# A loop over routed attention tiles: 33 tiles always and then pairs up to 39, in place of 32 always and then pairs up to 40

## The chip, the cores and the metric

The kernel runs on one core of a Trainium2 chip. The metric is the device time of one execution in microseconds. Three runs of the kernel before the change took 3995.53, 3995.71 and 4000.58 us; their median is 3995.71 us.

## What is computed

The reference is a sequence of eight sublayers over 2048 tokens of 128 channels, each added to its own input. The change lies in the sixth, a mixture of attention experts. For every token a small router picks two of eight experts. Each expert is a full attention over all 2048 tokens with 16 heads of 8 channels and its own weights; what it gives for a token is weighted by the router's gate. Cut to what matters:

```
probs = softmax(relu(layernorm(x @ rW1.T + rb1)) @ rW2.T + rb2)
tp, ti = top_k(probs, 2); tp = tp / tp.sum(-1)
for each expert e:                       # eight of them
    q, k, v = x @ W{q,k,v}[e].T + b      # 2048 tokens, 16 heads of 8
    o = softmax(q k^T * 8**-0.5) v
    out += (o @ Wo[e].T + bo[e]) * gate[token, e]   # gate 0 where e wasn't picked
```

An expert's output matters only for the tokens that picked it, so the kernel computes attention only for these (token, expert) pairs: 2 x 2048 = 4096 query rows in all.

## The kernel before, in words

**Lists and tiles.** `l2_router` counts how many tokens each expert got, and gives every expert as many tiles of 128 query rows as it needs, the last one of each filled up with blanks. The tiles of all experts stand one behind the other. `end[:, E - 1]` (lines 2173 to 2181) is the number of tiles needed. It lies between 32 (4096 / 128, nothing wasted) and 39. The list of query rows by tile is written to HBM by `l2_prepare`: first every entry is blanked with 0 (line 2289), then each pair's row is scattered to its slot (L2293). A blank entry thus means row 0. `l2_prepare` also computes queries, keys and values of all eight experts and stores them in HBM.

**The loop.** `attention_loop` (called by `l2_ffn` with `routed`) then works through the tiles. The instructions are written out for each tile and each engine; `each_tile` (lines 427 to 443) decides how many run. The first 32 bodies always run. Then every engine loads the number of rounds, which the router has computed, and two bodies at a time stand behind a comparison of it (L440): 16 rounds are the 32 tiles, and each round more is a pair of tiles, up to 40. So an even number of tiles runs, the smallest that holds those needed; a tile too many is computed from blanks and its result isn't used. The router's side is a chain on VectorE (lines 2179 to 2183): for each possible round n, is `end` greater than 2n, added up.

**One tile.** For 16 heads and all 2048 keys: a first pass of matmuls for the scores (TensorE, L666) whose maxima VectorE takes from PSUM (L908, 32 a tile), a second pass that gives the scores less their maximum (L691, 256 a tile), exponentials on ScalarE (L846, 64 a tile), and the weighted sum of the values (L712, 512 a tile). The first pass runs three of four groups of heads ahead of the second. Then a division on VectorE, two transpositions and the projection with the expert's output weights (L736), copied to `y` (L864) and stored by SyncE (L540). GpSimd splits the maxima and queries into bfloat16 parts (L598 to L605), loads the list of tile i + 2 (L1966) and gathers its queries with an indirect DMA (L1970); the gathered rows are transposed by TensorE (L749). SyncE loads keys (L288), values (L509), query parts (L480) and the maximum's rows (L489) for the tiles i + 1 and i + 2, whichever experts they belong to. Buffers alternate with the parity of the tile.

**The end.** The last step's values (L712), the division, transpositions and projection of the last tile stand behind the loop and go by the loaded number of tiles. SyncE waits there for every load it has issued, GpSimd for its gathers. `l2_collect` gathers each token's two results (L2407) from `expert_y_dram`, whose rows for tiles that might not run were blanked before (L2286).

Of the kernel before, what the change touches and what calls it, by code (L numbers as in the profile page):

```python
# [24 lines left out]
ALU = mybir.AluOpType  # L25
# [3 lines left out]
P = 128  # L29
T = 2048  # L30
# [367 lines left out]
def attention_loop(c, at, lead, tri=None, routed=None, keys_placed=None):  # L398
# [13 lines left out]
    tiles = routed.tiles if routed else NT  # L412
# [14 lines left out]
    def each_tile(eng, body):  # L427

        if not routed:
            for i in range(tiles):
                body(i)
            return tiles
        for i in range(2 * routed.least_rounds):
            body(i)
        rounds = eng.value_load(routed.rounds[0:1, 0:1], min_val=routed.least_rounds, max_val=tiles // 2)
        for r in range(routed.least_rounds, tiles // 2):
            with eng.If(rounds > r):  # L440
                body(2 * r)
                body(2 * r + 1)
        return rounds * 2

    def kx(tile):
        return at.kx[:, tile % 2 if routed else 0]
# [4 lines left out]
    q_loaded = [c.sem(f"attn_q_loaded{k}") for k in range(2)]  # L451
# [7 lines left out]
    if routed:  # L459
        k_loaded = [[c.sem(f"attn_k_loaded{k}{g}") for g in range(G)] for k in range(2)]  # L460
        v_loaded = [c.sem(f"attn_v_loaded{k}") for k in range(2)]
# [3 lines left out]
    QL = 16 * (2 * NR if routed else 2)  # L465
    KL = 16 * 2 * 2
# [3 lines left out]
    with nc.Block() as block:  # L470
        @block.sync
        def _(sp):
# [85 lines left out]
                load_max(g, 0)  # L558
            done = each_tile(sp, routed_loads if routed else tile_loads)
            if routed:  # L560
                pieces_ahead, pieces_placed = (done + 2) * (KL // 2), done * (KL // 2)
                sp.wait_ge(y_stored, done * 16)
                for g in range(G):
                    sp.wait_ge(max_loaded[g], done * ML + (ML if g < 2 else 0))
                for k in range(2):
                    sp.wait_ge(v_loaded[k], pieces_placed if k else pieces_ahead)
                    for g in range(G):
                        sp.wait_ge(k_loaded[k][g], pieces_placed if k and g == 3 else pieces_ahead)
                for k in range(2):
                    sp.wait_ge(q_loaded[k], done * (QL // 2) + QL)  # L570
                sp.wait_ge(s2_read, ring.read_when(done, 4))
                sp.dma_start(routed.y_dram[bass.ds(done, 1)].rearrange("a p d -> (a p) d"), routed.y[:, :]).then_inc(last_y_stored, 16)
                sp.wait_ge(last_y_stored, 16)
            else:
                for k in range(2):
                    sp.wait_ge(q_loaded[k], tiles // 2 * QL)
                for g in range(G):
                    sp.wait_ge(max_loaded[g], tiles * ML)

        @block.gpsimd  # L580
        def _(pool):
            g_ = nc.gpsimd

            class Link:


                def __init__(self):
                    self.k = 0

                def __call__(self, ins):  # L590
                    self.k += 1
                    ins.then_inc(pool_chain, 1)
                    pool.wait_ge(pool_chain, self.k)

            def same(dst, src):

                ones = at.one[:, :] if len(src.shape) == 2 else at.one[:, :].unsqueeze(2)
                return g_.tensor_tensor(dst, src, ones.to_broadcast(list(src.shape)), ALU.mult)  # L598

            def split(src, parts, rest, link, ready):  # L600

                link(same(parts[0], src))
                link(g_.tensor_tensor(rest, src, parts[0], ALU.subtract))
                link(same(parts[1], rest))
                g_.tensor_tensor(parts[2], rest, parts[1], ALU.subtract).then_inc(ready, 1)  # L605

            link = Link()

            def split_max(g, tile):
                pool.wait_ge(negm_ready, tile * G + (g + 1))  # L610
                split(at.negm[:, 4 * g:4 * g + 4].rearrange("p (a j) -> p j a", j=2), [at.mparts[:, g, :, n, :] for n in range(3)],
                      at.rest[:, g, :].rearrange("p (j a) -> p j a", j=2), link, mparts_ready)

            def split_q():
                split(routed.qT[:, :], [routed.qparts[:, n, :] for n in range(3)], routed.qrest[:, :], link, qparts_ready)

            if routed:
                for k in range(2):
                    if k:
                        pool.wait_ge(q_loaded[0], QL)  # L620
                    pool.wait_ge(first_q_copied, k + 1)
                    split_q()
            for g in range(lead):
                split_max(g, 0)

            def whole_tile(i):
                if routed:
                    routed.load_index(pool, i + 2, i % 2)
                for g in range(G):
                    group, tile = first_pass_of(i, g)  # L630
                    if routed and g == 0:
                        pool.wait_ge(routed.list_loaded, i * 16 + 48)
                        routed.gather(pool, i % 2)
                    if routed and g == 2:
                        pool.wait_ge(q_loaded[(i + 1) % 2], ((i + 1) // 2 + 1) * QL)
                        pool.wait_ge(s2_read, ring.read_when(i, ring.place(i, "q")))
                        split_q()
                    if exists(tile):
                        split_max(group, tile)

            done = each_tile(pool, whole_tile)
            if routed:
                for k in range(2):
                    pool.wait_ge(routed.gathered[k], done * 8 + 16)

        @block.tensor
        def _(pe):
# [1285 lines left out]
class Routed:  # L1933
# [7 lines left out]
    def __init__(self, c, ctx, E, K):  # L1941
        nc, sb = c.nc, c.sb
        self.E = E
        self.tiles = (K * T + E * (P - 1)) // P + 1
        self.listed = self.tiles + 2
        self.least_rounds = K * T // P // 2
        self.rounds = sb(ctx, "rounds", [1, 1], mybir.dt.int32)
        self.expert_of = sb(ctx, "expert_of_tile", [1, self.listed], mybir.dt.int32)
        self.q = sb(ctx, "gathered_q", [P, 2, P], F32)
# [43 lines left out]
def l2_router(c, ins, rt, E, K, gate, slot, row, y_row, fixed):  # L1993
# [3 lines left out]
    with ExitStack() as ctx:  # L1997
# [14 lines left out]
        first, end, index = c.sb(ctx, "first_tile", [P, E], F32), c.sb(ctx, "end_tile", [P, E], F32), c.sb(ctx, "partition", [P, 1], F32)  # L2012
        many = c.sb(ctx, "many", [P, 2], F32)
# [20 lines left out]
        with nc.Block() as block:  # L2034
# [83 lines left out]
            def _(dve):  # L2118
                v = nc.vector
# [56 lines left out]
                link(v.tensor_reduce(of_tile[:, :], passed[:, :], X, ALU.add))  # L2176
                v.tensor_scalar(of_tile[:, :], of_tile[:, :], float(E - 1), None, ALU.min).then_inc(of_tile_ready, 1)

                link(v.memset(many[:, 0:1], float(rt.least_rounds)))
                for n in range(rt.least_rounds, rt.tiles // 2):  # L2180
                    link(v.tensor_scalar(many[:, 1:2], end[:, E - 1:E], 2.0 * n, None, ALU.is_gt))
                    link(v.tensor_tensor(many[:, 0:1], many[:, 0:1], many[:, 1:2], ALU.add))
                link(v.tensor_copy(rt.rounds[:, :], many[0:1, 0:1]))

# [18 lines left out]
def l2_prepare(c, at, ins, rt, slot, row):  # L2203
# [6 lines left out]
    E, K = rt.E, 2  # L2210
    with ExitStack() as ctx:
# [1 line left out]
        bq, bv, bk = c.sb(ctx, "b_q", [P, 2, P], F32), c.sb(ctx, "b_v", [P, 2, P], F32), c.sb(ctx, "b_k", [P, 2], F32)  # L2213
        bq_ordered = c.sb(ctx, "b_q_head_order", [P, P], F32)
        wT = c.sb(ctx, "wT_qkvo", [P, 2, 4, P], F32)
        used = 2 * rt.least_rounds + 1
        blank_y, y_blanked = c.sb(ctx, "blank_y", [P, P], F32), c.sem("p_y_blanked")
        blank = c.sb(ctx, "blank_list", [rt.listed, P], mybir.dt.uint32)
        start = c.sb(ctx, "p_start_credit", [P, 10], F32)
# [559 lines left out]
```

## Time and profile before

| | us |
|---|---|
| median of three runs | 3995.71 |
| the profiled execution | 3996.37 |
| its span, first to last instruction | 3994.6 |
| TensorE busy in the span | 3278.7 (82%) |
| VectorE busy | 3026.2 (76%) |
| ScalarE busy | 2560.2 (64%) |
| GpSimd busy | 579.2 (14%) |
| mean granted clock of TensorE | 0.912 |

The profile is that of one execution; its times are us from the first instruction. PE is TensorE's matmuls and PEld its weight loads, DVE VectorE, ACT ScalarE, POOL GpSimd, SP SyncE; a "q" behind an engine's name means its sequencer, which branches, waits and issues DMAs while the engine itself stands idle. "L712" is a line of the kernel. An arrow `a<-b` reads "a written from b". "issue" as a releaser means that the engine waited for nothing that the profile shows. Names with `l2f_` belong to the sublayer of this change; the first sublayers use the same lines without it.

### The profile page before, as it was taken

What the parts mean: (1) busy time and instruction counts of PE and PEld (TensorE: products, weight loads), DVE (VectorE), ACT (ScalarE), POOL (GpSimd) and SP (SyncE); (2) the same over time, 40 slices, a digit from 0 to 9 for tenths busy, and PEclk for the clock granted to TensorE, in tenths of its full rate; (3) what the DMA queues carried; (4) which work ended last, traced back from release to release, by engine and by line L of the source; (5) the groups of instructions that cost most, each with busy time, mean ns of one, the idle gap of its engine ahead of it and who ended that gap; (6) DMA issues with size and microseconds to landing.
All of it is one profiled execution on the core that took longest, in us unless ns stands there. A gap on an engine that the chain in (4) does not pass through costs nothing. (4 is left out here: it accounts for less than half of the span.)

```text
span 3994.6 us, 130089 instructions
## 1 busy us (share of the span) xinstructions
PE 3278.7 (82%) x55226; PEld 2129.2 (53%) x55226; DVE 3026.2 (76%) x3768; ACT 2560.2 (64%) x4943; POOL 579.2 (14%) x1529
## 2 busy tenths in 40 slices
PE   2999999489997996464945559999999999999728
PEld 1666666235555674122434426666666666666414
DVE  5999999358893114997353459999999999999753
ACT  1899999347776343332211139999999999999622
POOL 0000000011000000563012011111111111111120
PEclk7999999779998998898957769999999999999858
DMA  4000000300000000530009864555545455455410
GB/s 115 9 7 9 9 7 5 98 17 11 9 7 2 22 21 27 179 137 6 1 22 172 243 157 118 127 125 123 128 122 130 120 128 127 120 126 120 107 34 11
DMA packets 209577, 305.80 MB, mean 77 GB/s; under 512 B 93116, under 2 KB 137602, under 8 KB 207950
## 3 DMA queue, kind: packets, MB, share of 16 engines
q1 hardware_dynamic: 202270, 286.06, 28.4%
q10 hardware_dynamic: 2048, 6.29, 0.8%
q8 instruction: 430, 7.05, 0.8%
q0 software_dynamic: 4688, 5.24, 0.6%
q14 instruction: 141, 1.16, 0.1%
HBM read 228.17 MB, written 60.40 MB: 72 GB/s over the span
## 5 line engine op out<-in xcount | busy, mean ns | idle before, releaser
L846 ACT ACTIVATE channels_qk<-psum 128x512 f32<-128x512 f32 (+1 forms) x3906 | 2101.0, 593 | 287.6 <-PE psum L691 201.8
L908 DVE TENSOR_REDUCE l2f_chunk_max<-psum 128x2 f32<-128x1024 f32 x1176 | 1359.7, 1218 | 53.2 <-PE psum L666 49.4
L908 DVE TENSOR_REDUCE chunk_max<-psum 128x2 f32<-128x1024 f32 (+2 forms) x832 | 918.6, 1158 | 105.5 <-PE psum L666 57.6
L666 PE MATMUL psum<-l2f_k_parts,l2f_q_parts 48*128 48x512 bf16 x2352 | 715.9, 388 | 37.7 <-DVE l2f_chunk_max L908 26.3
L691 PE MATMUL psum<-l2f_q_parts,l2f_k_parts 51*128 51x128 bf16 x9224 | 728.1, 218 | 3.7 <-issue 2.7
L712 PE MATMUL psum<-channels_qk,l2f_v_and_ones 128*9 128x128 f32 x18432 | 718.5, 274 | 13.3 <-issue 13.0
L691 PEld LDWEIGHTS psum<-l2f_q_parts,l2f_k_parts 51*128 51x128 bf16 x9224 | 496.9, 94 | 43.2 <-ACT channels_qk L846 38.9
L666 PE MATMUL psum<-k_parts,q_parts 48*128 48x512 bf16 (+3 forms) x1664 | 425.8, 382 | 109.6 <-DMA q_parts<-q_rows_dram 72.2
L712 PE MATMUL psum<-channels_qk,v_and_ones 128*9 128x128 f32 x12544 | 493.8, 276 | 1.7 <-ACT channels_qk L846 0.5
L712 PEld LDWEIGHTS psum<-channels_qk,l2f_v_and_ones 128*9 128x9 f32 x18432 | 396.8, 90 | 122.0 <-issue 15.7
L691 PE MATMUL psum<-q_parts,k_parts 51*128 51x128 bf16 x6272 | 431.4, 219 | 29.3 <-DMA q_parts<-minus_max_rows 10.4
L666 PEld LDWEIGHTS psum<-l2f_k_parts,l2f_q_parts 48*128 48x128 bf16 x2352 | 214.3, 94 | 303.8 <-DVE l2f_chunk_max L908 181.6
L691 PEld LDWEIGHTS psum<-q_parts,k_parts 51*128 51x128 bf16 x6272 | 286.3, 94 | 96.3 <-ACT channels_qk L846 61.0
L712 PEld LDWEIGHTS psum<-channels_qk,v_and_ones 128*9 128x9 f32 x12544 | 270.9, 90 | 82.2 <-ACT channels_qk L846 14.0
L666 PEld LDWEIGHTS psum<-k_parts,q_parts 48*128 48x128 bf16 x1664 | 122.1, 94 | 297.2 <-DVE chunk_max L908 152.0
L1663 PE MATMUL psum<-l1a_state_c,identity 128*128 128x512 f32 x256 | 125.9, 616 | 90.4 <-DVE l1a_state_c L1648 90.4
L598 POOL TENSOR_TENSOR l2f_minus_max_parts<-l2f_minus_max,l2f_one 128x4 bf16<-128x4 f32 x147 | 29.2, 199 | 1074.5 <-DVE l2f_minus_max L915 1074.5
L1362 DVE SCALAR_TENSOR_TENSOR x_normalised<-psum,l0f_expert_weights,x_normalised 128x128 f32<-128x128 f32 x128 | 36.1, 345 | 196.2 <-PE psum L1326 196.2
L598 POOL TENSOR_TENSOR minus_max_parts<-minus_max,one 128x4 bf16<-128x4 f32 x128 | 25.5, 199 | 976.6 <-DVE minus_max L915 976.6
L1614 ACT ACTIVATE psum<-l1a_delta,l1a_a 128x1024 f32<-128x1024 f32 x64 | 71.5, 1118 | 147.1 <-DVE l1a_input L1643 147.0
L1347 ACT ACTIVATE l0f_hidden<-psum,l0f_b_now 128x512 f32<-128x512 f32 x128 | 87.9, 687 | 118.3 <-PE psum L1317 118.3
L1663 PEld LDWEIGHTS psum<-l1a_state_c,identity 128*128 128x128 f32 x256 | 43.8, 189 | 172.2 <-DVE l1a_state_c L1648 139.2
(479 smaller groups left out, 3226.8 us busy)
## 6 DMA issues: line engine op xcount, KB each, us to landing
l2f_k_parts<-l2f_k_parts_dram SPq DMA_DIRECT2D x604, 192.0 KB, 3.5
l2f_v_and_ones<-expert_v_dram SPq DMA_DIRECT2D x148, 288.0 KB, 4.0
l1a_bc_rows<-ssm_rows_dram SPq DMA_DIRECT2D x32, 512.0 KB, 4.7
expert_v_dram<-l2f_v_and_ones SPq DMA_DIRECT2D x8, 1152.0 KB, 4.4
channels_qk<-ssm_rows_dram SPq DMA_DIRECT2D x16, 512.0 KB
expert_q_dram<-heads_out SPq DMA_DIRECT2D x8, 1024.0 KB, 7.5
l2f_q_parts<-l2f_gathered_q_parts SPq DMA_DIRECT2D x456, 16.0 KB
k_parts<-k_rows_dram ACTq DMA_DIRECT2D x32, 192.0 KB, 7.1
```

The source lines that it names most:

```text
L598: return g_.tensor_tensor(dst, src, ones.to_broadcast(list(src.shape)), ALU.mult)
L666: last = nc.tensor.matmul(c.ps[:, 2 * (n % 2) + j, 0:width], at.q[64 * j:64 * j + ROWS, tile % SLOTS, pair, :], kx(tile)[64 * j:64 * j + R ...
L691: last = nc.tensor.matmul(c.ps[:, ring.bank(i, place[j]), (2 * kk + pp) * P:(2 * kk + pp + 1) * P], kx(i)[64 * j:64 * j + ROWS + 3, pair, ...
L712: last = nc.tensor.matmul(oT[32 * m:32 * m + HD + 1, g * P:(g + 1) * P], vx(i)[:, kt, 4 * g + m, :], at.prob[:, s % 4, j, kk, pp * P:(pp + ...
L846: nc.scalar.activation(at.prob[:, s % 4, j, 0:kts, :].rearrange("p k q -> p (k q)"), c.ps[:, ring.bank(i, n), 0:kts * 2 * P], ACT.Exp, sca ...
L908: v.tensor_reduce(at.mx[:, 4 * g + 2 * pp:4 * g + 2 * pp + 2, chunk], c.ps[:, 2 * (n % 2):2 * (n % 2) + 2, 0:span.width(tile, chunk)], X, ...
L1347: nc.scalar.activation(mid[:, k % 2, f, :], ps[:, f, :], ACT.Gelu, bias=bnow[:, k // NC, f:f + 1]).then_inc(gelu_done, 1)
L1362: last = v.scalar_tensor_tensor(c.n[:, tile, :], ps[:, 4 + k % 2, t * P:(t + 1) * P], mix[:, tile, bass.ds(r * 2 + e, 1)], c.n[:, tile, :] ...
L1614: nc.scalar.activation(decay(step), delta[:, h, tokens(step)], ACT.Exp, scale=a[:, h, n:n + 1]).then_inc(da_ready, 1)
L1663: last = nc.tensor.matmul(ps[:, 2 * (step % 2) + b, :], c.ident[:, :], hc[:, step % U, b * 512:(b + 1) * 512], start=False, stop=step % S ...
```

## The change

The number of tiles that always run becomes 33, and the pairs behind comparisons are (33, 34), (35, 36) and (37, 38), so an odd number of tiles runs, up to 39. The router starts its count at 16 as before and adds one for n = 16, 17, 18 where `end` is greater than 2n + 1. `tiles`, the most there can be, goes from 40 to 39, and with it the lengths of the list and of `y` in HBM and the blanked rows of `y` (`used` goes from 33 to 34). What SyncE and GpSimd wait for behind the loop is rewritten for an odd number of tiles: which of the two buffers has had one load more. The body of a tile is the same.

```diff
--- before.py
+++ after.py
@@ -433,14 +433,14 @@
             for i in range(tiles):
                 body(i)
             return tiles
-        for i in range(2 * routed.least_rounds):
+        for i in range(routed.least):
             body(i)
-        rounds = eng.value_load(routed.rounds[0:1, 0:1], min_val=routed.least_rounds, max_val=tiles // 2)
-        for r in range(routed.least_rounds, tiles // 2):
+        rounds = eng.value_load(routed.rounds[0:1, 0:1], min_val=routed.least // 2, max_val=tiles // 2)
+        for r in range(routed.least // 2, tiles // 2):
             with eng.If(rounds > r):
-                body(2 * r)
                 body(2 * r + 1)
-        return rounds * 2
+                body(2 * r + 2)
+        return rounds * 2 + 1
 
     def kx(tile):
         return at.kx[:, tile % 2 if routed else 0]
@@ -558,16 +558,16 @@
                 load_max(g, 0)
             done = each_tile(sp, routed_loads if routed else tile_loads)
             if routed:
-                pieces_ahead, pieces_placed = (done + 2) * (KL // 2), done * (KL // 2)
+                pieces_ahead, pieces_placed = (done + 3) * (KL // 2), (done + 1) * (KL // 2)
                 sp.wait_ge(y_stored, done * 16)
                 for g in range(G):
                     sp.wait_ge(max_loaded[g], done * ML + (ML if g < 2 else 0))
                 for k in range(2):
-                    sp.wait_ge(v_loaded[k], pieces_placed if k else pieces_ahead)
+                    sp.wait_ge(v_loaded[k], pieces_placed)
                     for g in range(G):
-                        sp.wait_ge(k_loaded[k][g], pieces_placed if k and g == 3 else pieces_ahead)
-                for k in range(2):
-                    sp.wait_ge(q_loaded[k], done * (QL // 2) + QL)
+                        sp.wait_ge(k_loaded[k][g], pieces_placed if k or g == 3 else pieces_ahead)
+                sp.wait_ge(q_loaded[0], done * (QL // 2) + 3 * (QL // 2))
+                sp.wait_ge(q_loaded[1], (done * 2 + 2) * (QL // 4))
                 sp.wait_ge(s2_read, ring.read_when(done, 4))
                 sp.dma_start(routed.y_dram[bass.ds(done, 1)].rearrange("a p d -> (a p) d"), routed.y[:, :]).then_inc(last_y_stored, 16)
                 sp.wait_ge(last_y_stored, 16)
@@ -641,7 +641,7 @@
             done = each_tile(pool, whole_tile)
             if routed:
                 for k in range(2):
-                    pool.wait_ge(routed.gathered[k], done * 8 + 16)
+                    pool.wait_ge(routed.gathered[k], (done + (1 if k else 3)) * 8)
 
         @block.tensor
         def _(pe):
@@ -1941,9 +1941,9 @@
     def __init__(self, c, ctx, E, K):
         nc, sb = c.nc, c.sb
         self.E = E
-        self.tiles = (K * T + E * (P - 1)) // P + 1
+        self.tiles = K * T // P - 1 + E
         self.listed = self.tiles + 2
-        self.least_rounds = K * T // P // 2
+        self.least = K * T // P + 1
         self.rounds = sb(ctx, "rounds", [1, 1], mybir.dt.int32)
         self.expert_of = sb(ctx, "expert_of_tile", [1, self.listed], mybir.dt.int32)
         self.q = sb(ctx, "gathered_q", [P, 2, P], F32)
@@ -2176,9 +2176,9 @@
                 link(v.tensor_reduce(of_tile[:, :], passed[:, :], X, ALU.add))
                 v.tensor_scalar(of_tile[:, :], of_tile[:, :], float(E - 1), None, ALU.min).then_inc(of_tile_ready, 1)
 
-                link(v.memset(many[:, 0:1], float(rt.least_rounds)))
-                for n in range(rt.least_rounds, rt.tiles // 2):
-                    link(v.tensor_scalar(many[:, 1:2], end[:, E - 1:E], 2.0 * n, None, ALU.is_gt))
+                link(v.memset(many[:, 0:1], float(rt.least // 2)))
+                for n in range(rt.least // 2, rt.tiles // 2):
+                    link(v.tensor_scalar(many[:, 1:2], end[:, E - 1:E], 2.0 * n + 1.0, None, ALU.is_gt))
                     link(v.tensor_tensor(many[:, 0:1], many[:, 0:1], many[:, 1:2], ALU.add))
                 link(v.tensor_copy(rt.rounds[:, :], many[0:1, 0:1]))
 
@@ -2213,7 +2213,7 @@
         bq, bv, bk = c.sb(ctx, "b_q", [P, 2, P], F32), c.sb(ctx, "b_v", [P, 2, P], F32), c.sb(ctx, "b_k", [P, 2], F32)
         bq_ordered = c.sb(ctx, "b_q_head_order", [P, P], F32)
         wT = c.sb(ctx, "wT_qkvo", [P, 2, 4, P], F32)
-        used = 2 * rt.least_rounds + 1
+        used = rt.least + 1
         blank_y, y_blanked = c.sb(ctx, "blank_y", [P, P], F32), c.sem("p_y_blanked")
         blank = c.sb(ctx, "blank_list", [rt.listed, P], mybir.dt.uint32)
         start = c.sb(ctx, "p_start_credit", [P, 10], F32)
```

## Rows read from the trace of the kernel before

**Rows 1.** Page, costliest groups: form, count | busy us, mean ns | idle, releaser.
```profile
L908 DVE TENSOR_REDUCE l2f_chunk_max<-psum 128x2 f32<-128x1024 f32 x1176 | 1359.7, 1218 | 53.2 <-PE psum L666 49.4
...
L712 PE MATMUL psum<-channels_qk,l2f_v_and_ones 128*9 128x128 f32 x18432 | 718.5, 274 | 13.3 <-issue 13.0
```

**Rows 2.** Busy by stretch: us, PE, PEld, DVE, ACT, POOL, PEclk, DMA share, GB/s.
```profile
2430.00:3780.00 1350.00, 1320.28 (x28962) 906.96 (x28959) 1295.55 (x1307) 1233.13 (x2506) 217.02 (x756) 0.99 0.52 124
```

**Rows 3.** Line L749: count, shortest/median/longest ns, first and last start.
```profile
L749 PE MATMUL psum<-identity,l2f_gathered_q x36: 327/328/330, 2379.6 to 3740.8; 128*128 128x128 f32 x36
```

**Rows 4.** GpSimd timeline: start, us; gathers of tiles 26, 28, 34 to 37.
```profile
3301.69 0.99 POOL L1970 DMA_INDIRECT l2f_gathered_q<-expert_q_dram,l2f_gathered_index  x1 [2.35 <-DMA l2f_gathered_index<-query_list_dram]
...
3379.42 0.99 POOL L1970 DMA_INDIRECT l2f_gathered_q<-expert_q_dram,l2f_gathered_index  x1 [2.39 <-DMA l2f_gathered_index<-query_list_dram]
...
3614.11 0.99 POOL L1970 DMA_INDIRECT l2f_gathered_q<-expert_q_dram,l2f_gathered_index  x1 [2.19 <-DMA l2f_gathered_index<-query_list_dram]
...
3652.31 0.98 POOL L1970 DMA_INDIRECT l2f_gathered_q<-expert_q_dram,l2f_gathered_index  x1 [2.43 <-DMA l2f_gathered_index<-query_list_dram]
...
3691.45 1.00 POOL L1970 DMA_INDIRECT l2f_gathered_q<-expert_q_dram,l2f_gathered_index  x1 [2.02 <-DMA l2f_gathered_index<-query_list_dram]
...
3730.54 0.98 POOL L1970 DMA_INDIRECT l2f_gathered_q<-expert_q_dram,l2f_gathered_index  x1 [2.62 <-DMA l2f_gathered_index<-query_list_dram]
```

**Rows 5.** DMA view, 5 us behind each of those gathers, in the same order.
```profile
q0 software_dynamic: 32, 0.07, 4.4%
...
q0 software_dynamic: 32, 0.07, 16.4%
...
q0 software_dynamic: 32, 0.07, 6.0%
...
q0 software_dynamic: 32, 0.07, 16.0%
...
q0 software_dynamic: 32, 0.07, 16.5%
...
q0 software_dynamic: 32, 0.07, 13.8%
```

**Rows 6.** Line L440, branches by engine: shortest/median/longest ns, first and last start.
```profile
L440 ACTq COMPARE_BRANCH  x4: 34/47/50, 3607.2 to 3762.9; - x4
L440 PEldq COMPARE_BRANCH  x4: 65/2185/5144, 3607.8 to 3767.3; - x4
```

**Rows 7.** Waits from 3683 to 3690 us: total, times, longest, in us.
```profile
PEld psum L666 <- DVE l2f_chunk_max L908: 1.2, 4, 0.6
```

**Rows 8.** Timeline of the exit, all engines: start, us, idle before in brackets.
```profile
3772.63 0.60 PE L712 MATMUL psum<-channels_qk,l2f_v_and_ones 128*9 128x128 f32 x5 [9.18 <-issue]
...
3776.69 0.60 ACT L852 ACTIVATE l2f_out_channels<-psum 128x512 f32<-128x512 f32 x1 [8.25 <-PE psum L712]
...
3778.82 0.25 DVE L920 RECIPROCAL l2f_denominators<-l2f_out_and_denominators 128x16 f32<-128x16 f32 x1 [13.70 <-ACT l2f_out_and_denominators L859]
```

**Rows 9.** Timeline of VectorE in the router, from 2066 us.
```profile
2066.17 0.15 DVE L2181 TENSOR_SCALAR l2f_many<-l2f_end_tile 128x1 f32<-128x1 f32 x1
...
2066.55 0.15 DVE L2181 TENSOR_SCALAR l2f_many<-l2f_end_tile 128x1 f32<-128x1 f32 x1
```

**Rows 10.** Line L1970, what its engine sat idle for: us, times.
```profile
  DMA expert_q_dram<-heads_out: 150.5, 1
```

**Rows 11.** GpSimd timeline from 2082 us: the blanking of y.
```profile
2082.97 1.12 POOL L2286 DMA_DIRECT2D expert_y_dram<-l2f_blank_y  x1 [0.32 <-POOL l2f_blank_y L2283]
```

**Rows 12.** DMA queues around the exit, 3764.4 to 3776.7: packets, MB, share.
```profile
q8 instruction: 4, 0.07, 3.0%
q14 instruction: 5, 0.04, 1.2%
```

**Rows 13.** DMA queues over the loop, 2430 to 3780 us.
```profile
q8 instruction: 233, 3.82, 1.3%
...
q14 instruction: 80, 0.66, 0.2%
```

## The prediction

> **What bounds the kernel now.** The page comes first: of the work in the routed attention it counts 1176 of the long chunk maxima (L908, names with `l2f_`) and 18432 matmuls of the weighted values (L712) [rows 1]. One tile issues 32 and 512 of these in the code, so 18432 / 512 = 36 tiles ran in this execution; the maxima run three groups of 8 ahead, which is done once before the loop (32 x 36 + 24 = 1176). The table by stretch then shows what such a tile costs in kind: over 1350 us of the loop TensorE is busy 98% (1320.28), VectorE 96% (1295.55), ScalarE 91%, at a granted clock of 0.99 and with DMA engines half used [rows 2]. Nothing there can absorb a tile: it is paid by two engines that have no slack, whatever is in it. The view of one tile's transposition of gathered queries (L749) gives the period: 36 of them between 2379.6 and 3740.8 us, once a tile, so 1361.2 / 35 = 38.89 us a tile [rows 3]. These instructions don't look at whether a row of the tile is a real query or padding, so an empty tile costs 38.89 us too.
>
> **What decides is therefore a count.** Before, the loop runs an even number of tiles, 32 to 40: the smallest that holds the needed tiles. After, an odd number, 33 to 39. With N needed tiles, 36 run before only if N is 35 or 36; after, 35 run for N = 35 and 37 for N = 36. So the change is worth one whole tile, and its sign hangs on N alone.
>
> Two sources give N. First the reference: its own router on its own inputs (drawn with the default seed, float32) sends 2007, 463, 0, 463, 450, 2, 74 and 637 tokens to the eight experts, in all 2 x 2048. Rounded up to 128 that is 16 + 4 + 0 + 4 + 4 + 1 + 1 + 5 = 35. How firm is it? The count changes if expert 7 gets 4 tokens more (637 of at most 640), if expert 2 gets one, or if expert 5 loses both of its own; yet only one of the 2048 tokens has its second and third logit closer than 1e-4 together and none closer than 1e-5, so rounding in the chip's layers would have to be far off.
>
> Second, the trace, which I read as a test of that table. A blank entry of the list points to row 0, so a gather for an empty tile reads one row 128 times. Tile numbers count back from the last gather, which fetches for tile 37 (tiles are gathered two ahead) [rows 4]. In the 5 us behind each gather the software queue moves the same 32 packets and 0.07 MB, but their share of time differs [rows 5]: 16.5% and 13.8% for tiles 36 and 37, which are empty for certain; 6.0% for tile 34; 4.4% for tile 26, a full one by the table. Tile 35 shows 16.0%, so it looks empty. Tile 28 shows 16.4%: by the table that is where the expert with 2 tokens lies, 126 blanks of 128. So the table's order shows in the trace. The limit of this test: it can't tell an empty tile from one with two queries, and for that the reference's count is needed. I take N = 35.
>
> **The change part by part.**
> - *One tile less in the loop.* Removed from every engine are the 32 maxima, 843 matmuls and transpositions (512 at L712, 256 at L691, 64 at L666, 11 others), 64 exponentials and 9 copies, and from SyncE some 42 transfers (16 of keys, 4 of values, 12 of query parts, 8 of the maximum's rows, one each of y and the output weights), from GpSimd one index load, one gather and the splits. The loads two tiles ahead for a tile that never runs stay, now for tiles 35 and 36. At the period that is -38.89 us. Bounds by the unequal steps from gather to gather, 38.20 (tile 34 to 35) and 39.14 (35 to 36) [rows 4].
> - *One pair less to enter.* Before, the four comparisons of L440 are two entered (rounds 16 and 17) and two skipped (18, 19). After, with 17 rounds, one is entered (16) and two are skipped (17, 18). An entered one costs TensorE the 65 ns of the shortest L440 record, and nothing beyond what waits of that stretch look like anyway: the longest single wait of TensorE from 3683 to 3690 us is 0.6 us, on the maxima of VectorE, not on a branch [rows 6, 7]. I take -0.1 us, bounds 0 and -0.6. A figure of a page for this: the Trainium skill, "Advanced Engine Details and Errata" (Control Flow Timing), gives a compare-and-branch as about 108 ns; by it this term would still be 0.1 us.
> - *The exit.* The costly branches are the skipped ones: the four TensorE records of L440 are 65 ns at least, 5144 at most and 2185 in the middle, so the middle two sum to 4.37 us, one short and one of some 4.3 us. Together 4.3 + 5.1 = 9.4 us, which is the idle time of 9.18 us before the last values (L712) at 3772.63, with ScalarE (8.25) and VectorE (13.70) waiting behind them [rows 6, 8]. Two skips before, two skips after, each over bodies of two tiles as before: 0 us. Bounds: -1 and +1, since where the code falls relative to what is fetched may shift; the two skips of one trace differ by 0.9.
> - *The router.* The loop over possible rounds has three turns in place of four; a turn is two small VectorE operations, 0.38 us from start to start (2066.17 to 2066.55), in a chain where each waits for the last and on which the query list waits [rows 9]: -0.38 us. Bounds 0 and -0.4.
> - *Blanked rows and buffers.* y's blank rows go from 8 to 6, the list from 42 to 41. GpSimd issues them under the wait for the stored queries, 150.5 us at the first gather [rows 10]: 0. Without that cover at most the 1.12 us of the issue that writes them [rows 11]. The value of `rounds` is loaded once by each engine either way, and behind the loop SyncE waits for as many semaphores as before, with counts that fit an odd number of tiles.
>
> Sum: 38.89 + 0.10 + 0 + 0.38 = 39.4 us less. The profiled execution took 3996.37 us (span 3994.6 and 1.8 around it): 3957.0. It lies 0.7 above the median of the three runs, 3995.71, so the median after is forecast as 3956.3 us, 1.0% faster.
>
> **The rivals.**
> 1. *N is 36, so 37 tiles run.* The place is the count on the router's last row; it decides as soon as one expert crosses a multiple of 128. One tile more at 38.89; two pairs entered as before; one skip fewer, -4.3 to -5.1; router -0.38. That is +33.8 us: 4029.5. For it: tile 35 with one or two queries would look as it does in rows 5; against it: the reference's count and the lack of near ties. Chance 2%.
> 2. *The exit eats part of the gain.* A skip costs 4.3 to 5.1 us of TensorE waiting where an entered pair costs 0.07. If the new place of the code made each skip cost double, 9.4 us would come back: 3956.3 + 9.4 = 3965.7. For it: in the 12.3 us around the exit the two instruction queues bring 4 and 5 packets, where the 1350 us of the loop hold 233 and 80, so 2.1 and 0.7 in 12.3 us [rows 12, 13]; the stall looks like fetched code, and its size may hang on where the code lies. Against it: the bodies skipped are as long as before and there are as many. Beside it stands the Trainium skill, "Runtime: NRT & Kernel Launch" (Instruction fetch mechanics): branching away from the pages already fetched stalls until the target page has come. The trace agrees, with 4.3 and 5.1 us against 65 ns. Chance 4%.
> 3. *The change doesn't do what it says:* the new test `end > 2n + 1` or the odd start still yields 36 tiles' work. The test for n = 17 asks 35 > 35 and fails, so I see no way. Then the time would stay within a us of 3995.7. Chance 1%.
>
> **How the numbers follow.** Forecast 93%, rivals 4, 2 and 1%. Range of the forecast: bounds of the terms reach from 38.2 + 0 - 1 + 0 = 37.2 to 39.14 + 0.6 + 1 + 0.4 = 41.1 us less, so 3954.6 to 3958.5; the three runs of before spread over 5 us, mostly upwards, so I go to 3963 above and to 3952 below. Rivals lie outside and hold 7%. A measurement of this kernel can tell about 0.2%, 8 us, from no change. Faster by more than that: 93 + 4 = 97%; same 1%; slower 2%.
>
> **What would show it.** Right: 17920 of the values' matmuls (35 x 512), 1144 maxima, 35 transpositions at L749, one spacing of 38.9 us; three L440 branches on TensorE, two of them of 4 to 5 us; the exit's idle time before L712 near 9 us; three L2181 records; all stages behind the loop shifted by 39.4 us and alike in length. Wrong: 18944 values' matmuls (rival 1), L712's idle time near 18 us (rival 2), 18432 (rival 3), or a spacing of tiles that moved off 38.9.

## The result, and the profile after

The first comparison gave 3950.95 us in the median of four executions of the kernel after (3938.95 to 3957.81), against 3995.62 of four before: a ratio of 0.9883, with an interval of 0.9866 to 0.9901. That is 44.7 us less where 39.4 were forecast, and 1 us below the stated range. The direction and the term that carries most of it came as forecast; the whole size did not, and more executions moved it. In three comparisons the kernel after ran 14 times: median 3953.6 us, mean 3953.3, from 3938.95 to 3961.52, with a standard deviation of 5.6. The kernel before ran 63 times over all comparisons: median 3993.6, mean 3994.0, from 3983.70 to 4004.81, deviation 4.8. The difference of the means is 40.7 us, give or take 3.2 (twice the root of 5.6² / 14 + 4.8² / 63, which is 1.6).

The page after counts the work of 35 tiles, 1144 maxima and 17920 matmuls of the values, where [rows 1] had 36:

```profile
L908 DVE TENSOR_REDUCE l2f_chunk_max<-psum 128x2 f32<-128x1024 f32 x1144 | 1322.6, 1218 | 49.3 <-PE psum L666 45.5
...
L712 PE MATMUL psum<-channels_qk,l2f_v_and_ones 128*9 128x128 f32 x17920 | 697.5, 274 | 10.2 <-issue 10.1
```

The views of the lines L749, L440, L2181 and L2407 after (count, shortest, median and longest in ns, first and last start) answer to [rows 3, 6, 9] and show where the next stage begins:

```profile
L749 PE MATMUL psum<-identity,l2f_gathered_q x35: 327/328/330, 2361.6 to 3684.2; 128*128 128x128 f32 x35
...
L440 PEldq COMPARE_BRANCH  x3: 84/3951/4778, 3629.2 to 3710.4; - x3
...
L2181 DVE TENSOR_SCALAR l2f_many<-l2f_end_tile x3: 154/154/155, 2052.3 to 2053.1; 128x1 f32<-128x1 f32 x3
...
L2407 POOL DMA_INDIRECT heads_out<-expert_y_dram,l2f_y_row x16: 940/944/1061, 3724.2 to 3761.9; - x16
```

The period is (3684.2 - 2361.6) / 34 = 38.90 us, as before; one L440 record of TensorE is short and two are long. But three things stand there that the sum didn't have. The span of this execution is 57.4 us shorter than that of the first one of before (3937.2 against 3994.6), and 18.0 us of it lie ahead of the loop: the third query tile is transposed at 2361.6 in place of 2379.6 us. And from the last L749 to the first gather of the next stage it takes 3724.2 - 3684.2 = 40.0 us, where it took 43.7 before. This stretch is called the exit below. And from that gather to the end of the span it takes 213.0 us, where it took 210.2 before. With the loop between, 1361.2 against 1322.6 us, the 57.4 us are complete: 18.0 + 38.6 + 3.7 - 2.8, within rounding.

The timeline of the exit after, beside [rows 8] (start, duration, idle time before in brackets), shows the second:

```profile
3715.33 1.04 PE L712 MATMUL psum<-channels_qk,l2f_v_and_ones 128*9 128x128 f32 x16 [8.49 <-issue]
...
3716.44 0.60 ACT L852 ACTIVATE l2f_out_channels<-psum 128x512 f32<-128x512 f32 x1 [4.84 <-PE psum L712]
...
3718.56 0.25 DVE L920 RECIPROCAL l2f_denominators<-l2f_out_and_denominators 128x16 f32<-128x16 f32 x1 [10.05 <-ACT l2f_out_and_denominators L859]
```

The 16 matmuls of the last values run in one piece. In [rows 8] the line has x5. The other eleven stand in the next line of TensorE in the timeline of before, behind a second stop of 2.4 us that the prediction passed over:

```profile
3775.63 1.03 PE L712 MATMUL psum<-channels_qk,l2f_v_and_ones 128*9 128x128 f32 x11 [2.40 <-issue]
```

In that stop, from 3772.9 to 3775.6 us, the DMA view of before has one packet on q8, one of the two instruction queues:

```profile
q8 instruction: 1, 0.02, 2.2%
```

After, the waits of ScalarE (8.25 to 4.84) and VectorE (13.70 to 10.05) shrink by 3.4 and 3.7 us.

### The profile page after: what moved, and what is told of

Read it like the earlier page. It is cut to its first block and busy times, and to the rows that moved or that the text cites. A ratio compares the mean times of both kernels' runs of the same rounds, so it can differ in the third digit from the quotient of the medians.

```text
span 3937.2 us, 128114 instructions
## 1 busy us (share of the span) xinstructions
PE 3232.7 (82%) x54382; PEld 2095.8 (53%) x54382; DVE 2988.6 (76%) x3728; ACT 2524.2 (64%) x4870; POOL 573.1 (15%) x1507
## 5 line engine op out<-in xcount | busy, mean ns | idle before, releaser
L846 ACT ACTIVATE channels_qk<-psum 128x512 f32<-128x512 f32 x3842 | 2066.3, 593 | 280.4 <-PE psum L691 197.3
L908 DVE TENSOR_REDUCE l2f_chunk_max<-psum 128x2 f32<-128x1024 f32 x1144 | 1322.6, 1218 | 49.3 <-PE psum L666 45.5
L666 PE MATMUL psum<-l2f_k_parts,l2f_q_parts 48*128 48x512 bf16 x2288 | 696.0, 387 | 37.3 <-DVE l2f_chunk_max L908 25.9
L691 PE MATMUL psum<-l2f_q_parts,l2f_k_parts 51*128 51x128 bf16 x8968 | 707.7, 217 | 1.3 <-ACT l2f_minus_max_rows L888 0.4
L712 PE MATMUL psum<-channels_qk,l2f_v_and_ones 128*9 128x128 f32 x17920 | 697.5, 274 | 10.2 <-issue 10.1
L691 PEld LDWEIGHTS psum<-l2f_q_parts,l2f_k_parts 51*128 51x128 bf16 x8968 | 482.8, 94 | 40.2 <-ACT channels_qk L846 37.9
L712 PEld LDWEIGHTS psum<-channels_qk,l2f_v_and_ones 128*9 128x9 f32 x17920 | 385.5, 90 | 115.2 <-issue 11.9
```

The costliest lines, as they stand in the source:

```text
L666: last = nc.tensor.matmul(c.ps[:, 2 * (n % 2) + j, 0:width], at.q[64 * j:64 * j + ROWS, tile % SLOTS, pair, :], kx(tile)[64 * j:64 * j + R ...
L691: last = nc.tensor.matmul(c.ps[:, ring.bank(i, place[j]), (2 * kk + pp) * P:(2 * kk + pp + 1) * P], kx(i)[64 * j:64 * j + ROWS + 3, pair, ...
L712: last = nc.tensor.matmul(oT[32 * m:32 * m + HD + 1, g * P:(g + 1) * P], vx(i)[:, kt, 4 * g + m, :], at.prob[:, s % 4, j, kk, pp * P:(pp + ...
L846: nc.scalar.activation(at.prob[:, s % 4, j, 0:kts, :].rearrange("p k q -> p (k q)"), c.ps[:, ring.bank(i, n), 0:kts * 2 * P], ACT.Exp, sca ...
L908: v.tensor_reduce(at.mx[:, 4 * g + 2 * pp:4 * g + 2 * pp + 2, chunk], c.ps[:, 2 * (n % 2):2 * (n % 2) + 2, 0:span.width(tile, chunk)], X, ...
```

## Experiments

**Twice the same kernels.** `before_again` is the kernel before, `after_again` the kernel after, unchanged, and later once more as `after_third`. The question: does the change itself save the 18 us ahead of the loop, or do they come and go?

> The kernel before, unchanged, against itself. Theory A (the part of the gain ahead of the loop is a chance pattern of TensorE's granted clock in the mixed stages, which differs from execution to execution): the ratio is 1.000 within 0.2%, but the profiled execution places the start of the loop (first copy of the output channels, L852, 2402.6 us in the first trace of before) somewhere else by 3 us or more, with the loop's period 38.9 us and the exit (last two L852 copies 51.1 us apart) unchanged within 0.3 us. Theory B (the change itself saves some 15 us ahead of the loop): the start of the loop is again at 2402.6 within 3 us.

> The kernel after, unchanged. Theory A: 43 us below before in the median (38.9 for the tile, 3.7 for the exit, 0.4 for the router), so a ratio of 0.989; the profiled execution has the start of the loop anywhere between 2384 and 2405 us; the exit is again 47.4 us within 0.3. Theory B: the start of the loop is again near 2384.6 us and the ratio 0.986 or lower. The forecast as it stood: 39.4 us, a ratio of 0.990, exit at 51 us.

Measured: before against itself 1.0002 (0.9991 to 1.0012); after 0.9907 (0.9890 to 0.9923), 3954.28 us in six executions; theory A's 0.989 and the forecast's 0.990 both lie in that interval or at its edge. The third query tile is transposed at 2374.9 us in `before_again`, 4.7 earlier than in the first trace of the same kernel, and at 2370.7 and 2376.0 in the two further traces of after, where the first had 2361.6. So theory A holds, and the 18 us were mostly chance. Its second part was too strict: the distance of the last two copies of the output channels (L852), expected within 0.3 us of 51.1 and 47.4, came out at 51.7 and 48.7, so the exit too varies by more than a microsecond. Where the larger part of the 18 us comes from can be read in the table by stretch (us, then PE, PEld, DVE, ACT and POOL busy, granted clock, DMA share, GB/s). The router of the kernel before, in `before_again`, and below it the small router of the first mixture of experts, which the change doesn't touch:

```profile
2004.90:2077.10 72.20, 34.69 (x153) 29.85 (x153) 41.25 (x154) 11.42 (x19) 7.09 (x30) 0.52 0.04 7
...
1268.20:1299.40 31.20, 17.29 (x97) 13.86 (x97) 15.74 (x68) 8.60 (x13) 0.29 (x8) 0.67 0.02 2
```

The same two stretches in the first trace of after:

```profile
2002.40:2068.10 65.70, 28.62 (x153) 23.94 (x153) 40.93 (x152) 11.42 (x19) 7.11 (x30) 0.60 0.05 8
...
1267.00:1297.80 30.80, 16.82 (x97) 13.39 (x97) 15.75 (x68) 8.63 (x14) 0.30 (x8) 0.62 0.02 2
```

And in the first trace of before, the two stretches and no other:

```profile
2010.00:2082.30 72.30, 34.63 (x153) 29.79 (x153) 41.25 (x154) 11.43 (x19) 7.11 (x30) 0.52 0.04 7
...
1269.60:1305.70 36.10, 22.21 (x97) 18.77 (x97) 15.76 (x68) 8.62 (x13) 0.31 (x8) 0.51 0.01 2
```

The number of matmuls is the same, 153 and 97; VectorE's busy time too, but for the two small operations of the turn that the router saves. What differs is TensorE's time for them, 6.0 us in the router with a granted clock of 0.60 in place of 0.52, 4.9 us in the other between two executions of the same kernel (0.51 and 0.67). The granted clock of a stretch is the mean of two levels, 1.2 and 2.4 GHz: at 0.52 the lower one stood nearly throughout, at 0.60 the upper one a fifth of the time. In these stages TensorE works in short bursts with pauses (34.6 of 72.3 us), and how much of their work meets the upper level differs from one execution to the next; the router of `after_again`, the same kernel as after, is back at 34.65 us, 0.52 and 71.8 us. These two stretches make some 12 of the 18 us; the other 6 were not traced to a stage. The 210.2 or 213.0 us behind the exit come and go too: 210.5 in `after_again` and 212.7 in `before_nested`, with a cause that no run here shows. The steady part of the router is visible beside it: 72.3 and 72.2 us before (and 72.3 in a variant of before), 71.8 and 71.9 in the repeat of after and its variant. That is the 0.4 us of the saved turn.

> The kernel after once more, unchanged, beside the two below on one chip. Theory: 39.3 us for a tile and the router, plus 2 to 3.5 us at the exit, so a ratio to before between 0.989 and 0.990; start of the loop anywhere within 2384 to 2405 us; the stretch from the last L749 to the first L2407 40 to 41.5 us. The rival that the tile alone is gained and the exit nothing: 43.7 us there, ratio 0.9902.

Measured: 0.9897 (0.9881 to 0.9914), 3954.01 us. The stretch from the last L749 to the first L2407 took 40.9 us, 41.3 in `after_again`, 40.0 in the first; in the two traces of before 43.7 and 44.3. So the exit is 3.2 us shorter after, in the mean of each. The start of the loop (the first L852 at 2399.0 us), the exit and the ratio lie where they were expected; the ratio of the rival, 0.9902, lies in the interval as well, and only the exit speaks against it.

**Why the exit is shorter.** Two kernels move TensorE's code without changing its work. They add waits on a semaphore that has been reached, where TensorE idles behind the preparing stage. Two such waits make one instruction: the traces have 169 and 32 records of the line, 51 ns each, more than 1400 us ahead of the exit.

```diff
                 pe.wait_ge(w_loaded[0], LOADS)
                 transpose_weights(0)
                 each_expert(pe, project)
+                for _ in range(338):                 # after_shift169; 64 in before_shift32
+                    pe.wait_ge(w_loaded[0], LOADS)
```

The size comes from the trace: a tile is 1705 instructions on TensorE (844 weight loads, 844 matmuls, 17 waits); the loop of 1350 us, or 34.7 tiles, has 233 packets of 16 KB on queue q8 [rows 13], so 6.7 a tile and 254 instructions a packet. That fits 256. The kernel after is one tile shorter, 6 x 256 + 169 instructions.

> The kernel after with 338 waits on a semaphore that has long been reached, on TensorE, behind its last work of the preparing stage, where it idles for some 30 us: 169 instructions, which is by how much one tile's 1705 exceed six pages of 256. They move the code of the loop's end to where before has it within a page. Theory F (the exit is 3.7 us shorter after because no fetch of code falls into the last values): the idle time of 2.4 us between the 5th and the 16th of the last values (L712) comes back, and the last two L852 copies are 50.5 to 51.3 us apart in place of 47.4; median 3 to 4 us above the kernel after. Theory G (the exit is shorter for another reason, such as parity of the last tile or the length of the skipped code): it stays at 47.4 us. The added instructions themselves cost nothing, since TensorE waits there for the gathered queries.

> The kernel before with 64 such waits, 32 instructions, at the same place. Theory F: the page's end moves out of the last values, the idle time of 2.4 us there goes, and the last two L852 copies are 47 to 48.5 us apart in place of 51.1; median 3 us below before, ratio 0.9992. Theory G: 51.1 us as before.

Timeline of TensorE and ScalarE at the exit of `after_shift169`:

```profile
3729.80 0.60 PE L712 MATMUL psum<-channels_qk,l2f_v_and_ones 128*9 128x128 f32 x5 [9.83 <-issue]
3733.68 1.03 PE L712 MATMUL psum<-channels_qk,l2f_v_and_ones 128*9 128x128 f32 x11 [3.28 <-issue]
...
3734.75 0.60 ACT L852 ACTIVATE l2f_out_channels<-psum 128x512 f32<-128x512 f32 x1 [9.15 <-PE psum L712]
```

And of `before_shift32`:

```profile
3768.60 1.04 PE L712 MATMUL psum<-channels_qk,l2f_v_and_ones 128*9 128x128 f32 x16 [9.06 <-issue]
...
3769.70 0.60 ACT L852 ACTIVATE l2f_out_channels<-psum 128x512 f32<-128x512 f32 x1 [4.77 <-PE psum L712]
```

The stop comes back in the kernel after, behind the same fifth matmul as in [rows 8], and goes from the kernel before. Between the last two copies of the output channels it is now 52.6 us after (47.4, 48.7 and 48.3 unshifted) and 48.0 before (51.1 and 51.7); for after 50.5 to 51.3 had been expected, and what lies above it is a stop of 3.3 in place of 2.4 us and a longer wait ahead of it. Theory F is shown, against theory G: whether the stop is there hangs on where the code lies, and 169 or 32 instructions decide. All 13 traces fit: of the kernel before and its variants, those whose code wasn't shifted stop behind the fifth matmul (2.4 to 2.9 us), and of the kernel after and its variants only the shifted one does. That the stop is a wait for fetched code rests on this and on the packet of q8 that lies in it; such a packet also comes in `before_shift32` (at 3769.28), beside running matmuls and without a stop. The medians could not have shown any of this: 3956.66 us for `after_shift169`, 2.4 above `after_again` where 3 to 4 were expected, and 3993.97 for `before_shift32`, 1.1 above before where 3 below were expected; ratios 0.9913 (0.9897 to 0.9930) and 1.0003 (0.9993 to 1.0013). The Trainium skill, "Runtime: NRT & Kernel Launch" (Instruction fetch mechanics), states that code is fetched in blocks of 16 KiB, 256 instructions, ahead of the execution; the packets' size and the effect of a shift by 169 agree.

**The count as a lever.** `after_37` and `before_34` change only the start of the router's count of rounds, by +1 and -1. The second leaves out the 35th tile, with the last 125 queries; it is there for its time alone:

```diff
-                link(v.memset(many[:, 0:1], float(rt.least // 2)))
+                link(v.memset(many[:, 0:1], float(rt.least // 2 + 1)))        # after_37
```

> The kernel after with the number of rounds one higher: 37 tiles run, the two last of them empty. It is the case of the first rival of the prediction. Theory: two tiles of 38.9 us more, one entered pair more (0.1) and one jump less (4.3 to 5.3): 73 us above the kernel after, so 4026 us where after stands at 3953, and a ratio to before of 1.008; 39 L440 records aside, TensorE shows one long one. A rival: an empty tile is cheaper than a full one, since its gather reads one row; then less than 68 us.

> The kernel before with the number of rounds one lower: 34 tiles run, and the 35th, with the last 125 queries, is left out. Theory: two tiles less (77.8), one entered pair less (0.1), one jump more (4.3 to 5.3): 73 us below before, a ratio of 0.982, three long L440 records on TensorE. Beside the kernel after, which runs one tile more with two jumps: one tile and a jump apart, so 34 us below it, plus or minus the 3 us of a page's end in the last values.

Measured: 4025.13 us, 1.0082 (1.0068 to 1.0097), and 3918.47 us, 0.9813 (0.9801 to 0.9826). The view of L440 in `after_37` has one long record:

```profile
L440 PEldq COMPARE_BRANCH  x3: 65/84/3821, 3640.5 to 3795.3; - x3
```

and in `before_34` three (4.1, 4.9 and 4.7 us, one after the other):

```profile
L440 PEldq COMPARE_BRANCH  x4: 84/4392/4917, 3614.1 to 3700.7; - x4
```

The two kernels are three tiles apart, 106.7 us, and their exits (38.6 and 48.2 us from the last L749 to the first L2407) differ by 9.6 the other way: (106.7 + 9.6) / 3 = 38.8 us a tile, give or take 2 by the spread of five and six executions. The trace is sharper: in `after_37` the copies of the output channels of the 35th tile and of the 36th, an empty one, lie 38.85 us apart, as those of full tiles do. An empty tile is no cheaper. `before_34` came 35.1 us below the kernel after (3953.6), where 34 were expected. `after_37` is also what the first rival would have been: 4025.1 against 4029.5 worked out for it, of which 2.1 us is that the three executions the sum started from lay above the median of all (3995.7 against 3993.6).

**One jump in place of two.** The loop's comparisons nested:

```diff
-        for r in range(routed.least // 2, tiles // 2):
-            with eng.If(rounds > r):
-                body(2 * r + 1)
-                body(2 * r + 2)
+        def rest(r):
+            if r < tiles // 2:
+                with eng.If(rounds > r):
+                    body(2 * r + 1)
+                    body(2 * r + 2)
+                    rest(r + 1)
+
+        rest(routed.least // 2)
```

> The kernel after with each pair's comparison standing inside the pair before it, so that the first pair that isn't run is the only jump: one branch over four bodies in place of two over two bodies each. Theory H (each jump of TensorE past code costs 4 to 5 us, whatever its length): one long L440 record of 4 to 5.3 us in place of two, ScalarE's and VectorE's waits shorter by as much, the last two L852 copies 43 us apart (48.0 less 4.9) if no page ends in the last values, 46 if one does; median 4 to 5 us below the kernel after. Theory I (the cost goes with the length jumped over): one record of 9 to 10 us and no gain.

> The same nesting in the kernel before: 36 tiles, one jump over four bodies. Theory H: the last two L852 copies 46.5 us apart in place of 51.4 (the page's end in the last values stays about where it is), median 4 to 5 us below before. Theory I: 51.4 us.

The lines behind it stand five lower: the comparison is L442, the projection L741. The view of L442 in `after_nested`:

```profile
L442 PEldq COMPARE_BRANCH  x2: 84/1908/3732, 3646.7 to 3725.8; - x2
```

One long record of 3.7 us over four bodies, where two over two bodies took 4.0 and 4.8 (5.3 and 4.7 in the repeat): theory H, the price is one of the jump and not of its length. In the kernel before, the exit fell from 44.0 to 38.7 us by it, and the median was 3990.35, 2.4 below before where 4 to 5 were expected, a ratio of 0.9990 (0.9978 to 1.0002). In the kernel after it fell only from 40.8 to 38.5, median 3951.80, 0.9895 (0.9878 to 0.9911), not to be told from after, where 4 to 5 us had been expected. The distance of the last two L852 copies did fall as expected, to 42.4 us and in the kernel before to 46.2, so the rest was lost behind them. The waits of `after_nested` at the exit say what took the rest:

```profile
PEld psum L741 <- DMA l2f_w_out_now<-expert_w_out_dram: 4.0, 1, 4.0
PE psum L741 <- DMA l2f_w_out_now<-expert_w_out_dram: 3.7, 1, 3.7
```

The last output weights stand on SyncE's queue behind the query parts for a tile that never runs. With two jumps TensorE came late enough to find them there or nearly so: a wait of 0.7 us of its weight loads stands in the first trace of after, and it stands in `after_third` as well, put down to nothing there. With one jump it waits. The next two kernels move them forward:

```diff
                     load_values(i + 1, g, following)
+                    if g == 3 and i > 0:
+                        sp.wait_ge(s2_read, ring.read_when(i, ring.place(i, "proj")))
+                        sp.dma_start(routed.y_dram[i], routed.y[:, :]).then_inc(y_stored, 16)
+                        load_w_out(this)
                     if g == 3:
                         load_q(i + 2)
                     after_step(i, 8 * g + 7)
                     load_pair(keys_of[0], keys_of[1], 1, keys_of[2])
-                    if g == 3 and i > 0:
...
```

> The kernel after with y's store and the load of the output weights moved ahead of the twelve transfers of query parts on SyncE's queue. Theory J (with two jumps TensorE comes late enough that the last output weights have landed or nearly so: TensorE waited 0.7 us for them): 0 to 0.7 us at the exit, no difference that can be told in the median. A rival: the query parts, now some 1.5 us later in every tile, reach the first pass late; then the loop's period rises above 38.95 us.

> Both: one jump in place of two, and the output weights ahead of the query parts. Theory J (with one jump TensorE waited 3.7 us at the projection for the output weights, which ate most of what the nesting gave): that wait goes, the stretch from the last L749 to the first L2407 is 34.5 to 35.5 us in place of 38.5 (nested) and 40.1 to 41.4 (after); median 5 to 6 us below the kernel after. A rival: something else on SyncE's queue, y's own store or the last key loads, is late next, and 2 us or more of it stay.

`after_early`: 3955.24 us, 0.9902 (0.9885 to 0.9918), exit 40.2, as theory J has it. The period is 38.95 us, at the edge of what the rival there asked for; `before_again` has the same, and a single wait of TensorE for query parts, 1.2 us at 2600.5, is all that the trace shows of it. `after_nested_early`: 3952.73 us, 0.9895 (0.9879 to 0.9912), but its exit took 40.1 us, not 35, and 1.7 more than with the nesting alone: the rival won. SyncE's timeline there:

```profile
3713.72 7.58 SPq L485 DMA_DIRECT2D l2f_q_parts<-l2f_gathered_q_parts  x10
3721.49 0.86 SPq L288 DMA_DIRECT2D l2f_k_parts<-l2f_k_parts_dram  x2
3727.14 0.39 SPq L577 DMA_DIRECT2D expert_y_dram<-l2f_y  x1
```

and ScalarE's copy of the last y in the same kernel:

```profile
3721.68 0.28 ACT L869 ACTIVATE l2f_y<-psum 128x128 f32<-128x128 f32 x1 [1.05 <-PE psum L741]
```

The projection no longer waits; y is ready at 3721.96 us. But SyncE is still issuing loads for tiles that don't run, jumps itself past the bodies (3722.4 to 3726.0 without an instruction of its own), and stores y only at 3727.14, 5.2 us late. ScalarE isn't far from the bound either: it stands still for 3.5 us behind its own comparison, and what TensorE's last values wait for in this trace is put down to ScalarE (4.0 us) and no longer to nothing. Issuing that store from ScalarE's queue would be the next step; it wasn't tried. None of the nested or reordered kernels beats the kernel after by what can be measured.

## Why the prediction was right or wrong

- **N = 35** was right: 17920 matmuls of the values, 35 tiles. It carried the sign and nine tenths of the amount, and the trace of before alone, with its gathers of one row, could not have decided it against 36 with one or two queries. The gathers show that only a tile of nearly all blanks stands out: the tiles 27 and 29, with 62 and 54 blanks by the table, took 6.6 and 9.2% over 5 us behind their gathers (from 3340.1 and 3418.2 us) where full or nearly full ones took 4.4 to 6.2%.
- **One tile, 38.89 us**: right. The period was 38.90 after, and the three tiles between `before_34` and `after_37` give 38.8 each by whole executions. (A tile has 844 matmuls, 12 others in place of the 11 of the prediction; nothing hangs on it.)
- **One pair less to enter, 0.1 us**: the record is gone (three in place of four); its size lies below everything measured here.
- **The router, 0.38 us**: right, 0.4 between the stretches at equal clock. Blanking and waits behind the loop: nothing of them shows.
- **The exit, "0 us. Bounds: -1 and +1"**: this is the step that failed. Two jumps stayed two jumps, of the same size (8.7, 9.4 and 10.0 us together after, 9.4 and 9.7 before). But the prediction priced the jumps alone and read the exit's stop as the one before the first five values; the second stop, 2.4 us, stood in the next line for TensorE and wasn't counted. Whether it is there hangs on the length of all code ahead of it, which the removed body shortens by 169 instructions beyond whole blocks. Measured: -3.2 us at the exit, beyond the bound of -1 that stood for a shift of the code. The idea of rival 2, that the exit changes with the place of the code, was thus right with the wrong sign: as a rival I had weighed only that it could grow.
- **"All stages behind the loop alike in length"** was wrong for the pair of first traces, 210.2 and 213.0 us; executions of both kernels or of their variants have either (210.5 in `after_again`, 212.7 in `before_nested`), so the change isn't what makes it.
- **The sum** becomes 38.9 + 0.1 + 3.2 + 0.4 = 42.6 us, which the 40.7 plus or minus 3.2 of all executions hold. They hold the forecast's 39.4 as well; only the traces tell the two apart.
- **The range, 3952 to 3963**, rested on three executions of before that lay within 5 us. Sixty-three span 21 us. A median of four has a deviation of some 3 us from that alone, and a 3.2 us error of the sum and a chance of 3 us together reach past the bound of 3952. The three executions also put the start of the sum 2.1 us above the median of all of before; with both mended the forecast is 3956.3 - 3.2 - 2.1 = 3951.0. That the first four executions of after gave just this, 3950.95, is luck: the median of all 14 is 3953.6, which lies inside the range.

## What to carry to other kernels

Where a loop's count is rounded up to what the code offers, work out the count that the data needs: where the steps begin can be worth a whole tile, here 1%, and with the wrong start it costs one, as `after_37` showed, 0.8% above before. For a set of tokens that needs an even number of tiles the two kernels should swap places; no such set was run. At the end of such a loop, read every stop of the exit down to the last store, not only the largest: behind TensorE's jumps stood a second stop, behind that the output weights, and behind those SyncE's own queue, each hidden by the one before. And before a range is drawn from a few executions, look for stages where the granted clock of TensorE changes in mid-stage; their time is not a constant of the kernel.

## What the hardware showed unexpectedly

- A jump past unexecuted code cost TensorE 3.7 to 5.3 us each, for two bodies of a tile or four; entering the code cost 65 to 86 ns.
- Straight code behind a jump stopped once more, for 2.4 to 3.3 us, 12 instructions behind the jump's target, and 32 or 169 instructions more than 1400 us earlier moved this out or in. In the loop itself no such stop shows in any trace, though 6.7 packets of q8 come for each tile: the longest idle time of TensorE's matmuls there is 0.7 us, but for the 1.2 us for query parts in `after_early`.
- The same 153 matmuls of the router took TensorE 34.7 us at a granted clock of 0.52 and 28.6 at 0.60, and the stage 71.8 or 65.7 us, in two executions of the kernel after (`after_again` and the first); a stage that the change doesn't touch gave 36.1 and 31.2 us in two executions of one kernel.
- A gather with 126 or all of its 128 indices on the same row took its queue 14 to 17% of the 16 engines' time over 5 us, where full tiles took 4 to 6% and those with 54 and 62 blanks 9 and 7% [rows 5].
